# A two-layer graph network with norms on one core: counters loaded by the block, own rows on a falling schedule, comparisons set inside the subtraction, and another split pattern

## The reference

```python
# stage 0: GCN, residual, layer norm
deg = segment_sum(1, dst) + 1;  dinv = rsqrt(deg)
h = dinv * (segment_sum((dinv * x)[src], dst) + dinv * x) @ W + b + (t_emb @ Wt + bt)
x = layernorm(x + h)
# stages 1 and 2: two SAGE layers, residual, layer norm
h1 = relu(mean_over_dst(x[src])  @ Wl1.T + x  @ Wr1.T + b1)
h2 =      mean_over_dst(h1[src]) @ Wl2.T + h1 @ Wr2.T + b2
out = layernorm(x + h2)
```

## Time and profile before

| | |
|---|---|
| median of 3 runs | 3669.81 us (3665.44 to 4489.61) |
| profiled execution: time | 3676.87 us |
| its span, first to last instruction | 3674.9 us |
| its mean granted TensorE clock | 0.945 |
| PE busy | 3181.8 us, 87% |
| DVE busy | 1919.1 us, 52% |
| ACT busy | 1050.7 us, 29% |
| POOL busy | 2435.1 us, 66% |
| stage 0 / 1 / 2, first to last gather starts | about 153 to 1193 / 1239 to 2378 / 2417 to 3638 us |

### The profile page before, as it was taken

How to read it: one execution, slowest core, us unless ns; L and a number is a source line. 1 busy time by engine, 2 the same in 40 slices (tenths; PEclk the granted TensorE clock), 3 DMA queues, 4 the chain that set the end, 5 groups by cost and what they waited for, 6 DMA issues and landing times.

```text
span 3674.9 us, 73564 instructions
## 1 busy us (share of the span) xinstructions
PE 3181.8 (87%) x9570; PEld 1625.4 (44%) x9571; DVE 1919.1 (52%) x5738; ACT 1050.7 (29%) x1526; POOL 2435.1 (66%) x2365
## 2 busy tenths in 40 slices
PE   7378889999999799999888889968889888888887
PEld 7133444444444344444444444434444444444444
DVE  8333344454444355554655666635455456555665
ACT  0311112222222222223333333322222233333343
POOL 0377777777666376665777777646656567777674
PEclk9788999999999899999989999989999998889999
DMA  4777777777766566666777777766655567766664
GB/s 157 251 207 211 212 218 231 231 239 230 217 211 203 169 201 190 189 176 192 209 223 227 226 228 236 223 186 196 200 168 176 166 179 207 207 177 197 189 198 145
DMA packets 257091, 744.01 MB, mean 202 GB/s; under 512 B 44188, under 2 KB 45758, under 8 KB 256792
## 3 DMA queue, kind: packets, MB, share of 16 engines
q0 software_dynamic: 187680, 615.14, 58.1%
q10 hardware_dynamic: 57276, 105.62, 8.1%
q1 hardware_dynamic: 11868, 20.99, 1.7%
HBM read 688.67 MB, written 53.71 MB: 202 GB/s over the span
## 4 chain that ended last, share of the span: by engine, by line
PE 55%; issue 17%; DMA 9%; POOL 7%; ACTq 3%; ACT 3%; DVE 2%; DVEq 2%; POOLq 0%; SPq 0%
PE sum_ps L891 33%; PE prod_ps L898 10%; DMA raw<-table,idx_ring 8%; PE root_ps L898 7%; POOL raw L373 7%; DVE raw L609 1%; ACTq L210 1%; ACT hi L746 1%; PE aggT_ps L871 1%; PE sum_ps L859 1%; DVEq L210 1%; PE root_ps L906 1%; PE selfT_ps L913 1%; ACTq L214 1%; DMA selfbuf<-table 1%
## 5 line engine op out<-in xcount | busy, mean ns | idle before, releaser
L373 POOL DMA_INDIRECT raw<-table,idx_ring x2346 | 2419.6, 1031 | 1113.1 <-issue 685.3
L891 PE MATMUL sum_ps<-raw,oh 128*128 128x512 f32 x3528 | 1520.7, 558 | 57.3 <-issue 36.1
L609 DVE TENSOR_TENSOR raw<-raw,hi 128x256 fp32r<-128x256 f32 x2352 | 840.9, 420 | 610.0 <-ACT hi L746 609.5
L746 ACT ACTIVATE hi<-raw 128x1024 fp32r<-128x1024 f32 x588 | 619.6, 1057 | 1733.3 <-SPq L297 1408.7
L574 DVE TENSOR_SCALAR oh<-iota_row,tile_base,dst_tab 128x128 fp32r<-128x128 bf16 x2352 | 717.5, 354 | 687.8 <-issue 473.5
L891 PEld LDWEIGHTS sum_ps<-raw,oh 128*128 128x128 f32 x3528 | 676.0, 198 | 592.1 <-issue 523.4
L891 PE MATMUL sum_ps<-hi,oh 128*128 128x512 f32 x1176 | 520.1, 524 | 251.5 <-DVE raw L609 192.5
L898 PE MATMUL prod_ps<-W,aggT 128*128 128x512 f32 x1176 | 547.5, 609 | 17.0 <-ACT aggT L671 16.6
L891 PEld LDWEIGHTS sum_ps<-hi,oh 128*128 128x128 f32 x1176 | 208.9, 196 | 486.1 <-issue 480.5
L898 PE MATMUL root_ps<-W,selfT 128*128 128x512 f32 x800 | 393.5, 637 | 0.0
L898 PEld LDWEIGHTS prod_ps<-W,aggT 128*128 128x128 f32 x1176 | 222.0, 194 | 277.2 <-issue 269.3
(11 more groups left out here) (125 smaller groups left out, 1199.8 us busy)
## 6 DMA issues: line engine op xcount, KB each, us to landing
selfbuf<-table ACTq DMA_DIRECT2D x152, 256.0 KB
raw<-table,idx_ring POOLq DMA_INDIRECT x2346, 3.8
table<-stage ACTq DMA_DIRECT2D x7, 1792.0 KB, 6.7
table<-X ACTq DMA_DIRECT2D x49, 256.0 KB, 4.2
table<-hbuf ACTq DMA_DIRECT2D x49, 256.0 KB
X<-table ACTq DMA_DIRECT2D x49, 256.0 KB
X<-in_x SPq DMA_DIRECT2D x6, 2048.0 KB
out<-X ACTq DMA_DIRECT2D x48, 256.0 KB
```

The costliest lines, as they stand in the source:

```text
L373: nc.gpsimd.indirect_dma_start(out=raw[:, n, j, :], out_offset=None, in_=tables[L][:, :], in_offset=bass.IndirectOffsetOnAxis(ap=idx_ring[ ...
L609: last = v.tensor_tensor(lo[:, n, j, cols], raw[:, n, j, cols], hi[:, k, j, cols].bitcast(fp32), ALU.subtract)
L746: a.activation(hi[:, k, :, :], raw[:, n, :, :], ACT.Copy).then_inc(S["hi_ready"], 1)
L891: last = mm(bank, of[:, j, :], half[:, j, :], start=fresh, stop=False, skip_group_check=True)
```

## The change

- `ended` and `rooted` are loaded at the start of a block: nine counters by one call (and three of `rooted` in stages 1 and 2), without the run-time test of the bounds. `ended` has two zeros more in front. The first value of a loop over tiles is masked (`& TILE_BITS`).
- The rounds of own rows are due by a square: T + 1 - T(1 - (w + 1)/(0.75 NW))^2 before window w, held at T + 1 from 75% of the windows on. The rate starts at 1.33 a window and falls to nothing.
- VectorE makes the comparisons of the **next** group while it works on a group, set between three subtractions of 344, 336 and 344 columns. The signal `rows_ready` of a following unsplit group is given with them.
- Split slots: in stage 0 slots 0 and 4 for blocks 0 to 28, all but slot 7 for blocks 29 to 48 (two loops one after the other); in stages 1 and 2 all but 2 and 5.
- ScalarE keeps its distance of two groups the other way round: it rounds group n and does the tile ends of group n - 2, but own rows at group n. The last block isn't written out any more; two groups' tile ends follow the loop. `next_indices` moves to the end of the block.

The diff, cut to its core:

```diff
-    SPLIT = ((0, 4), (0, 2, 3, 5, 7), (0, 2, 3, 5, 7))
-    PIECE = D // 2
+    PIECES = ((0, 344), (344, 680), (680, CH * D))
+    FEW, MOST, NEARLY = (0, 4), (0, 1, 3, 4, 6, 7), (0, 1, 2, 3, 4, 5, 6)
+    SECTIONS = (((0, 29, FEW), (29, NBLK, NEARLY)), ((0, NBLK, MOST),), ((0, NBLK, MOST),))
+    HIS = len(NEARLY)
...
-    ROOT_RATE = T / (0.4 * NW)
+    ROOT_WINDOWS = 0.75 * NW
...
+        def rounded(n):
+            return hi[:, n if n < HIS else 2, :, :]
...
-        def ended_before(eng, g):
-            return eng.value_load(ended[0:1, bass.ds(g, 1)], min_val=0, max_val=T)
+        def ended_before(which, g, groups):
+            return nc.values_load_multi_w_load_instructions(
+                ended[0:1, bass.ds(g + LEAD, groups + 1)], engines=[which], min_val=0, max_val=T,
+                skip_runtime_bounds_check_because="a count of the T tiles, made by a sum of T comparisons")[1]
...
             with eng.If(end > first):
-                with eng.Fori(first, end) as t:
+                with eng.Fori(first & TILE_BITS, end) as t:
...
-            link(v.tensor_scalar(rooted_w[:, 1:2], iota_s[:, 0:1], 1.0, ROOT_RATE, ALU.add, ALU.mult))
+            link(v.tensor_scalar(rooted_w[:, 1:2], iota_s[:, 0:1], -1.0 / ROOT_WINDOWS, 1.0 - 1.0 / ROOT_WINDOWS,
+                                 ALU.mult, ALU.add))
+            link(v.tensor_scalar(rooted_w[:, 1:2], rooted_w[:, 1:2], 0.0, None, ALU.max))
+            link(v.tensor_tensor(rooted_w[:, 1:2], rooted_w[:, 1:2], rooted_w[:, 1:2], ALU.mult))
+            link(v.tensor_scalar(rooted_w[:, 1:2], rooted_w[:, 1:2], float(-T), float(T + 1), ALU.mult, ALU.add))
...
-                with dve.Fori(0, NBLK) as b:
-                    end = ended_before(dve, b * SLOTS)
+                def one_hots(g, n, tile):
+                    dve.wait_ge(S["pe_done"], g + (NG * L + 1))
+                    for j in range(CH):
+                        yield one_hot(oh[:, n, j, :], g * CH + j, tile)
+                def part(n, cols):
+                    rows, high, low = (of.rearrange("p c d -> p (c d)")[:, cols[0]:cols[1]]
+                                       for of in (raw[:, n, :, :], rounded(n), lo[:, n, :, :]))
+                    return v.tensor_tensor(low, rows, high.bitcast(fp32), ALU.subtract)
+                def groups(b, first_block, split, hi_base):
+                    ends = ended_before(mybir.EngineType.DVE, b * SLOTS, SLOTS)
+                    if L > 0:
+                        rounds = rooted_before(mybir.EngineType.DVE, b)
                     for n in range(SLOTS):
...
-                        first, end = end, ended_before(dve, g + 1)
-                        dve.wait_ge(S["pe_done"], g + (NG * L + 1))
-                        one_hot(oh[:, n, 0, :], g * CH, first)
-                        last = one_hot(oh[:, n, 1, :], g * CH + 1, first)
+                        following = one_hots(g + 1, (n + 1) % SLOTS, ends[n + 1])
+                        unsplit_next = (n + 1) % SLOTS not in split
                         if n in split:
...
-                            for j in range(CH):
-                                for c in range(0, D, PIECE):
...
+                            part(n, PIECES[0])
+                            next(following)
+                            part(n, PIECES[1])
+                            next(following)
+                            part(n, PIECES[2]).then_inc(S["rows_ready"], 1 + unsplit_next)
+                        else:
+                            next(following)
+                            last = next(following)
+                            if unsplit_next:
+                                last.then_inc(S["rows_ready"], 1)
+                        each(dve, ends[n], ends[n + 1], lambda t1: tile_end(g, t1))
...
+                def groups(b, first_block, split, hi_base):
+                    ends = ended_before(mybir.EngineType.Activation, b * SLOTS - LEAD, SLOTS)
+                    if L > 0:
+                        rounds = rooted_before(mybir.EngineType.Activation, b)
                     for n in range(SLOTS):
...
+                        if n in split:
+                            act.wait_ge(S["gathered"], b * SLOTS + (NG * L + n + 1))
+                            a.activation(rounded(n), raw[:, n, :, :], ACT.Copy).then_inc(S["hi_ready"], 1)
                         if L > 0 and n % HR == 0:
...
+                            each(act, rounds[n // HR], rounds[n // HR + 1], lambda r: own_rows(L, r), T + 1)
+                        each(act, ends[n], ends[n + 1], lambda t1: tile_end(L, t1))
+                    act.wait_ge(S["gathered"], b * SLOTS + (NG * L + SLOTS))
+                    next_indices((b + L) % 2, (b + 2) % NBLK)
...
-                with act.Fori(0, NBLK - 1) as b:
-                    groups(b, False)
-                groups(NBLK - 1, True)
+                ends = ended_before(mybir.EngineType.Activation, NG - LEAD, LEAD)
+                for n in range(LEAD):
+                    each(act, ends[n], ends[n + 1], lambda t1: tile_end(L, t1))
```

106 lines of the change are left out of this document (48 added, 58 removed).

## The result

The changed kernel takes 3424.66 us (median of 4 runs, 3419.67 to 3429.04) beside 3669.1 for the kernel before: a ratio of 0.9336, 95% interval 0.9314 to 0.9359 (the ratio leaves out the one run of before in the slow state, 4489.61). It is 6.6% faster, by 244 us. The profiled execution has a span of 3417.9 us, 257 less than the 3674.9 of before. The prediction was 3485, in a range of 3400 to 3630.

The account below looks back on a forecast made before the run. GpSimd's gathers set most blocks, TensorE the end of stage 0, neither alone the first twenty blocks of stages 1 and 2. Stage 0 -21, stage 1 -64, stage 2 -103, together -188: 3485 us, range 3400 to 3630.

Parts of the forecast that it names:

- Floor, and who sets the time: Every stage: undisturbed gathers on GpSimd follow each other every 1.25 us, so a block takes at least 20.0 to 20.1.
- rival D: Rounds due in pairs still stop all engines; blocks 1 to 36 in stages 1-2 stay at 24.5; 3630 us; chance 0.08.
- The seams: Comparisons between VectorE's subtractions let a gather in after one piece; a split group then costs GpSimd 0.12 us.
- the square rule: A gather's wait grows as the square of a piece's length; three pieces cost 0.3 of before, 0.1 us a split group.
- Rival A: Comparisons let no gather in; a split group costs GpSimd 0.34 to 0.45 us; 3600 us; chance 0.18.
- The schedule: Own rows due at a falling rate fit beside the gathers; stage 1 blocks take 23.5, then 22, then 21.3 us.
- the 2.4 of mutual waits: Stage 1, blocks 1 to 20: 2.4 us a block above TensorE's need, engines waiting for each other; expected not to vanish.
- ScalarE's refetch: Stage 2: the 3.8 us from ScalarE's loop branch to its first instruction goes with a shorter body; 0.8 a block left.
- Rival B: The instruction refetch moves to VectorE's loop in stage 2, adding 3.5 us a block; 3560 us; chance 0.09.
- The split pattern: Each further split group saves TensorE 0.7 us; stage 0's blocks 36 to 47 go from 24.0 to 22 us.
- Counters: Head of each block: loading 12 counters costs about 2 us, hidden, so no term of its own.
- Rival C: Each counter still costs 0.65 us, all in one piece, 7.8 a block on VectorE; slower, 3860 us; chance 0.07.

## Why the prediction was right, and which terms were off

**Floor, and who sets the time.** The floor of 20.1 with 0.25 for each of six split groups gives 21.6, and blocks 21 to 47 of stages 1 and 2 took 21.6 and 21.9. The 0.25 comes from the same gathers, so this says only that nothing else is needed to fill the block. The account by the gathers' spacing held; rival D, in which rounds in pairs still stop everything, is out: blocks 1 to 20 took 22.0.

**The seams.** Mechanism right, size off by two: 0.25 a split group where I took 0.12 (the square rule). The trace shows a small reason: in the new pattern split groups stand side by side, so that the third piece of one and the first of the next form a run of two. VectorE's timeline, and a gather that it holds for 1.48:

```profile
955.85 0.94 DVE L618 TENSOR_TENSOR raw<-raw,hi 128x344 fp32r<-128x344 f32 x2
```
```profile
956.12 1.48 POOL L388 DMA_INDIRECT raw<-table,idx_ring  x1 [0.30 <-issue]
```

70 gathers were held so in the changed kernel, 33 with the old pattern in stages 1 and 2, 7 in the kernel before with seams, which paid (2309.2 - 2217)/588 = 0.16, near my 0.12. But each of the 70 waits only some 0.43 longer for it, 30 us of the 100 by which 786 x 0.25 exceeds 786 x 0.12. The larger reason is the price that I scaled: 0.34 is what a run cost in the kernel before, where many gathers escaped it, as told below. In the surroundings of the changed kernel the same run costs 0.60, and pieces of 0.50 us and not 0.45 give, by the same rule, 3 x (0.50/1.42)^2 x 0.60 = 0.22, an estimate; measured 0.23 with the old pattern ((2349.6 - 2217)/588). So the sign that I had named, a mean of 0.99 for stage 1's gathers, failed: it is 445.17/434 = 1.03. The other, no gather of 2 us, came true.

**Rival A.** Its mechanism, a hold through the whole row of subtractions, is real and was measured by taking the seams away: 3598, and I had written 3600. That nearness is partly luck: a split group cost 0.50 where I had 0.40, and blocks of stage 1 took 23.5 for 23.0, but those of stage 2 took 23.1 for 23.8. The rival fell only on whether a comparison ends the hold.

**The schedule.** I had 23.5, 22 and 21.3 us for the blocks of stage 1; it took 22.2 in blocks 1 to 12, and 21.9 and 21.5 behind them. I had kept the 2.4 of mutual waits where need and floor are equal; most of it went. Not through the schedule alone: with the old one the first twelve blocks still take 22.7 (24.8 before), and the seams alone bring them to 24.0. The counters gave nothing. What gave the rest is not shown: ScalarE's new order (tile ends two groups later, rounding at its own group) and the last block that is no longer written out were undone in no run, and are the rival that stays untested. By this term stage 1 came out better than forecast, -76 for -64, in spite of the dearer seams.

**ScalarE's refetch.** It went, as said, but my reason, the length of the body, was wrong: the same body moved by 24 instructions runs without it. That it went was luck in so far as the new loops happened to lie well; on VectorE 12 instructions more would have set it off. I had priced it at 38 of the 76 us by which stage 2 was slower (76 - 47 x 0.8), and it was 53. Stage 2 came out at 1033, not 1074; that is the largest error of the sum, though the dearer part of it (12 blocks at 22.4 for 24.3) is the mutual waits again. Rival B had this on VectorE at 75 us (3560 for 3485); set off by 12 moved instructions it cost 111. So the length of 312 at which VectorE's loop of before showed no pause was no safe measure, as the loop of 275 paused.

**The split pattern.** Stage 0's last twelve blocks took 21.9 for 22 forecast. But blocks 5 to 28, which I left unchanged, went from 20.3 to 20.5 (5 us), as in the kernel before with seams alone, and 29 to 35 took 21.7 for 20.9. I gave stages 1 and 2 a gain from the sixth split group, and it is a loss: TensorE saves 0.7 where it isn't what is waited for, and each further split group costs the gathers 0.25.

**Counters.** No term of their own, and two experiments found none. Rival C's 7.8 a block for the head was 2.8 on VectorE, and loading one by one saved nothing beyond the noise.

**Edges.** I had no term for the passages between stages, and they gave 16 of the 26 us outside the windows. With the old pattern in stage 0 the first of them stays at 46, so the new pattern there removes 11 of it, most likely TensorE's backlog at the end of stage 0, where TensorE was busy all the time before. The 5 us of the second, the 5 behind the last gather, and the other 5 are unexplained.

**The sum.** Forecast -188, measured -257 on the profiled execution: stage 0 -11 for -21, stage 1 -76 for -64, stage 2 -144 for -103, outside the windows -26 for nothing. That the time fell inside the range was in part luck, as errors of opposite sign met: the seams cost the gathers 100 us more than forecast, and waits that I had kept, the refetch and the passages gave back more than that. With 0.12 a split group and all else as it came out, the time would have been near 3330, below the range (an estimate: 100 us of gathers at the 175 for 192 below). (The edge of the range had a slip: a kernel at 20.8 in all blocks of stages 1 and 2 is 94 x 20.8 = 1955 for 2110, another -155 and not -130.)

**What no single part shows.** Undone from the changed kernel, seams, schedule, pattern and counters are worth 178, 44, 3 and -3; added to the kernel before, the seams are worth 30 and the loop's place 53. The parts aren't additive, and the likely reason is that each block waits for the last of three: gathers, TensorE, the sequencers. Shorter gathers pay little while rounds crowd the first twenty blocks: 110 us less of gathers bought 44 of the span there. Once these are spread and the refetch is gone, most of a hold is paid: 192 us more of gathers cost 175 of the span, with the pieces together.

**The same four pieces, 0.34 and 0.60.** The kernel before held gathers less than the changed kernel with the old pattern and four pieces together. In before, of the gathers that the first piece held, 59 ended with that piece and 38 with the run; with four together in the changed kernel none and 105. The pieces follow each other equally closely in both. What differs in the traces is what VectorE did just before the run. The run of the earlier trace rows came straight behind two comparisons. Others came after VectorE had waited for `hi`, as here (VectorE, then the gather):

```profile
707.15 1.43 DVE L609 TENSOR_TENSOR raw<-raw,hi 128x256 fp32r<-128x256 f32 x4 [3.33 <-ACT hi L746]
```
```profile
707.32 1.08 POOL L373 DMA_INDIRECT raw<-table,idx_ring  x1 [0.30 <-issue]
```

This gather ends at 708.40, 0.83 after the first piece (707.57), and not after the run. So it is throughout before: of the gathers held by one of the first three pieces, all 112 in runs that VectorE began after idling ended with their own piece, and 165 of 171 in runs begun without a gap ended with the run. Before with ScalarE's loop moved shows 119 of 119, and 171 of 178. In before 256 of 588 runs began after idling. With the comparisons put first they stand between the wait for `hi` and the run, and no run does; the page of the old pattern with four pieces together has 0.0 us of idle time ahead of the subtractions, where the earlier trace rows has 610.0:

```profile
L618 DVE TENSOR_TENSOR raw<-raw,hi 128x256 fp32r<-128x256 f32 x2352 | 836.1, 416 | 0.0
```

This is read from the traces; no run changes the gap alone.

**Open.** Some gathers get in inside a run begun without a gap: the 51 (most started 0.27 us into the piece) in the first of three pieces together, and 36 and 18 in the third of four pieces together. What ScalarE's new order is worth, why the waits of the first twenty blocks went beyond the schedule's share, why starts drift into the last piece with a third seam, and why a loop's place matters stay open too.

## What to carry to other kernels

Where a gather on GpSimd sets the pace, look at what VectorE does when gathers start: put an instruction with one input that has to be done anyway between those with two, rather than making them shorter, and don't let two such groups touch. A single column is enough to open a seam, but adding one for its own sake made this kernel slower. Price an extra split by what it costs the gathers as well as by what it saves TensorE, stage by stage. If a loop shows a pause of some 4 us at its branch and instruction packets, first move it by a few instructions, and read the packets again after every edit that changes the program's length; and expect that a fix is worth little until what binds beside it is gone.

## What was not expected of the hardware

- Back-to-back subtractions hold a gather as one when VectorE began them without a gap: 286 of 286 that were held by the second of three pieces waited for the third, and in before 165 of 171. After an idle stretch of VectorE they don't: 112 of 112 got in at the end of their own piece. The Trainium skill, SBUF — State Buffer, § SBUF: two separate sides, has the lock for one instruction; here the measurement decides, and the hold mostly lasts for the row, until a one-input instruction. Whether it is one lock or several in a row that GpSimd never wins was not told apart.
- A held gather ends 0.82 us after what held it (0.81 to 0.84 for all gathers over 1.1 us that ended behind a piece, in four kernels: before, after, three pieces together, and the old pattern with four together), whether it waited for one piece or for four.
- A place in the program is worth 53 us on ScalarE and 111 on VectorE, at the same loop length.
- TensorE's granted clock was 0.93 to 1.00 in the windows after, 0.92 to 1.00 before, and 0.950 and 0.945 over the profiled executions, so it doesn't tell the two kernels apart.
